# The exponential of the later routing softmaxes: GpSimd raises e to a power, in place of ScalarE's Exp

## The chip, the cores and the metric

One core of a Trainium2 chip runs the whole kernel. The metric is the device time of one execution in microseconds (us). Three runs of the kernel before are shown, and one execution was profiled.

## What is computed

Four residual layers on x of shape (4, 512, 128), each behind a layer norm: a gated power attention, a mixture of experts, a gated linear recurrence (HGRN), and the same mixture of experts again. The change lies in the routing of the mixtures. Cut to that:

```python
scores = softmax(xf @ gate_w.T, axis=-1)          # 8 experts
_, sel = top_k(scores + expert_bias, 2)
top_scores = take_along_axis(scores, sel, axis=1)
# rows sorted by expert; routed = x[token] * score
h = silu(routed @ w1[e]) * (routed @ w3[e])
out = zeros.at[token].add(h @ w2[e])
```

## The kernel before, in words

The 2048 tokens are worked in halves of 1024. A mixture layer on one half is one **set of jobs**, so there are four sets, m = 0 to 3 (two layers by two halves). A set has 23 jobs; a job is 128 gathered rows of one expert. All four sets run in one unrolled stream of 92 jobs (`for J in range(...)`, with `m, s = divmod(J, 23)`; s is the job's slot in its set).

One job goes through the engines like this. GpSimd gathers the 128 rows (`gather_pool`, L1518), twelve buffers deep. TensorE turns them (L1583), multiplies by w1 (L1614) and w3 (L1617). ScalarE takes silu of the first product (`silu_scalar`, L1693), VectorE multiplies it with the second product (`mix_vector`, L1757), TensorE turns the result (L1579), ScalarE copies what was turned (L1595), TensorE multiplies by w2 (L1634), ScalarE takes the product out of PSUM (L1700), and GpSimd returns it by an indirect DMA to the tokens' places (`return_pool`, L1526), eight buffers deep. TensorE's w1 product of a job waits until silu of the job before has emptied its bank, and silu of job J stands in ScalarE's queue ahead of the take-out of job J - 2.

Every engine works strictly in the order in which its instructions are written. What isn't part of a job is put between jobs by hand, by tables of slots (`IN_FIRST`, `IN_SECOND`, `IN_THIRD`): `between_tensor`, `between_vector`, `between_scalar` and `between_pool` are called behind each job and issue what their table has for that slot.

While set m runs, the routing of set m + 1 is prepared in this way. On VectorE the stages stand in the order `softmax` (L1370, L1371: the maximum over 8 experts and the subtraction, on the logits that TensorE left by L1322, a tile L8 of 128 x 64), `top` (L1374 to L1377: sum, reciprocal, product, bias), `first` and `second` (the two largest), and then ranks, slots and row numbers for the gathers. Between `softmax` and `top` stands the exponential: in the kernel before, `prepare_scalar(m, "exp")` on ScalarE (L1345), which waits for `s_rd` from VectorE and signals `s_re`, for which `top` waits. There are three such **places** within the jobs: in set 0 at slot 8 (`top` stands one slot later, behind the next job's L1757), in set 1 at slot 18, and in set 2 at slot 15 (there `softmax`, `top` and `first` all stand in the one slot, ahead of the next job's L1757). The exponential of the very first routing is made earlier, amid the attention layer, and isn't touched.

GpSimd's own stream within the jobs is, for each job, its return, then `between_pool`, then the gathers that are due. `norm_root` (L196) and `rms_pool` (L1945) there raise variances to the power -0.5 on tiles of 128 x 4; both are tensor_tensor with the operation pow.

`const_pool` makes the constants at the start; `s_const` counts them up to `NCONST`, for which VectorE waits before the first softmax and GpSimd before `key_rows_pool(True)`.

Of the kernel before, what the change touches and what calls it, by code (L numbers as in the profile page):

```python
# [1 line left out]

# [7 lines left out]
ALU = mybir.AluOpType  # L10
# [4 lines left out]
P = 128  # L15
# [8 lines left out]
NE, HID = 8, 352  # L24
# [3 lines left out]
HT = NT // 2  # L28
# [39 lines left out]
def build(nc, x, W, Wi, Wf, Wg, conv_i, conv_f, gnw, Wo, gate_w, ebias, w1, w2, w3, out):  # L68
# [8 lines left out]
    with ExitStack() as ctx:  # L77
        def sb(name, shape, dt=F32):
            return ctx.enter_context(nc.sbuf_tensor(name, shape, dt))

        def sem(name):
            return ctx.enter_context(nc.semaphore(name))
# [14 lines left out]
        carry1 = sb("carry1", [P, NE, HT])  # L97
        zeros = sb("zeros", [P, C])
        mhalf = sb("mhalf", [P, HT])
        iolane = sb("iolane", [P, P])  # L100
        idhi = sb("idhi", [P, 1])
        idlo = sb("idlo", [P, TOPK, HT])
# [15 lines left out]
        s_const = sem("s_const")  # L118
# [17 lines left out]
        def link(ins, who="dve"):  # L136

            count[who] += 1
            engine, done = own[who]
            ins.then_inc(done, 1)  # L140
            engine.wait_ge(done, count[who])

        def bc(ap, shape):
            return ap.to_broadcast(shape)
# [9 lines left out]
        def norm_turn(n, b):  # L154

            return norm_number(n, b) + 1

        def batch(b):
            return slice(TB * b, TB * b + TB)

        def by_scalar(n, b):
            return n == 1 and b < 3
# [29 lines left out]
        def norm_root(n, b):  # L192

            g = nc.gpsimd
            g.wait_ge(s_var, norm_turn(n, b))
            ins = g.tensor_tensor(lnr[:, batch(b)], lnv[:, batch(b)], mhalf[:, 0:TB], ALU.pow)  # L196
            if by_scalar(n, b):
                link(ins, who="pool")
                ins = g.tensor_tensor(shift[:, batch(b)], mneg[:, batch(b)], lnr[:, batch(b)], MUL)
            ins.then_inc(s_std, 1)  # L200
# [29 lines left out]
        def turn_scalar(n, b, bank):  # L230
            a = nc.scalar
            a.wait_ge(s_xTp, norm_number(n, b) + 1)
            a.activation(xT[:, 512 * b:512 * b + 512], ps[:, bank, :], ACT.Copy).then_inc(s_xT, 1)
# [5 lines left out]
        L8 = sb("L8", [P, HT, NE])  # L239
# [52 lines left out]
        def key_rows_pool(odd):  # L292

            g = nc.gpsimd
            if not odd:
# [4 lines left out]
                return  # L300
            g.wait_ge(s_const, NCONST)
            g.wait_ge(s_vzp, B)
# [106 lines left out]
        def unit_of(b):  # L409
            return 0 if b == 0 else 1  # L410

        NCONST = 17
        PARTS = 8
        STORES = 16 * 8

# [122 lines left out]
        def const_pool():  # L538
            g = nc.gpsimd

            def part1(t, v):
                link(g.memset(t[:], v), who="pool")

            def triangle(t, op, fill, base, pattern, cm):
                g.affine_select(out=t[:], in_=t[:], compare_op=op, fill=fill, base=base,
                                pattern=pattern, channel_multiplier=cm).then_inc(s_const, 1)

            part1(ident, 0.0)
            triangle(ident, ALU.not_equal, 1.0, 0, [[-1, P]], 1)
            part1(tri, 1.0)  # L550
            triangle(tri, ALU.is_ge, 0.0, 0, [[1, P]], -1)
            g.memset(zeros[:, :], 0.0).then_inc(s_const, 1)
            g.memset(onesb[:, :], 1.0).then_inc(s_const, 1)
            g.memset(ones[:, :], 1.0).then_inc(s_const, 1)
            g.memset(va[:, :, :, HS:VW], 1.0).then_inc(s_const, 1)
            link(g.memset(mhalf[:, :], -0.5), who="pool")
            norm_root(0, 0)
            part1(identb, 0.0)
            triangle(identb, ALU.not_equal, 1.0, 0, [[-1, P]], 1)
            part1(negmask, 0.0)  # L560
            triangle(negmask, ALU.is_ge, NEG, 0, [[0, TB], [1, P]], -1)
            for b in range(1, B):
                norm_root(0, b)
            key_rows_pool(False)
            part1(trib, 1.0)
            triangle(trib, ALU.is_ge, 0.0, -1, [[1, P]], -1)
            g.iota(iom8[:, :], [[1, NE]], base=-8, channel_multiplier=0, allow_small_or_imprecise_dtypes=True).then_inc(s_const, 1)
            g.iota(iojob[:, :], [[1, JOBS]], base=0, channel_multiplier=0, allow_small_or_imprecise_dtypes=True).then_inc(s_const, 1)
            g.iota(io128[:, :], [[P, HT]], base=0, channel_multiplier=0, allow_small_or_imprecise_dtypes=True).then_inc(s_const, 1)
            g.iota(iolane[:, :], [[1, P]], base=0, channel_multiplier=0, allow_small_or_imprecise_dtypes=True).then_inc(s_const, 1)  # L570
            g.iota(idhi[:, :], [[1, 1]], base=HT * TOPK, channel_multiplier=HT * TOPK, allow_small_or_imprecise_dtypes=True).then_inc(s_const, 1)
            g.iota(idpad[:, :], [[P, JOBS]], base=HT * TOPK * (P + 1), channel_multiplier=1, allow_small_or_imprecise_dtypes=True).then_inc(s_const, 1)
            g.iota(idlo[:, :, :], [[1, TOPK], [TOPK, HT]], base=0, channel_multiplier=0, allow_small_or_imprecise_dtypes=True).then_inc(s_const, 1)
            part1(carry1, 1.0)
            g.memset(carry1[:, :, 0:1], 0.0).then_inc(s_const, 1)
            key_rows_pool(True)
            for n in range(NOFF):
                decayed_pool(0, n)
# [582 lines left out]
        def heads_pool():  # L1161
            g = nc.gpsimd
            for G in range(GROUPS):
                for r in range(GH):
# [38 lines left out]
        s_rd = sem("s_rd")  # L1203
        s_re = sem("s_re")
# [53 lines left out]
        IN_FIRST = {'stats': 4, 'apply': 6, 'turn': 7, 'logits': 8, 'softmax': 8, 'exp': 8, 'top': 9, 'first': 10, 'second': 11,  # L1258
                    'ranks': 12, 'weigh': 12, 'slots': 13, 'spread': 15, 'lanes': (15, 16), 'number': 17, 'ids': 17, 'experts': 19,
                    'taps': 19, 'root': 1, 'high': 16}  # L1260
# [80 lines left out]
        def prepare_scalar(m, stage):  # L1341
            a = nc.scalar
            if stage == "exp":
                a.wait_ge(s_rd, m + 1)
                a.activation(L8[:], L8[:], ACT.Exp).then_inc(s_re, 1)  # L1345
            if stage == "high":
                a.wait_ge(s_eq, m + 1)
                a.activation(injobid[:, :, 0, :], injob[:], ACT.Copy, scale=idhi[:, 0:1]).then_inc(s_in, 1)

        def prepare_vector(m, stage):  # L1350
# [12 lines left out]
            if stage == "softmax":  # L1363

                v.wait_ge(s_lgp, m + 1)
                if m == 0:
                    v.wait_ge(s_eb, 16)
                    v.wait_ge(s_const, NCONST)
                lgt = ps[:, BK_X, 0:64].rearrange("p (t e) -> p t e", e=NE)
# [350 lines left out]
        def between_scalar(m, s):  # L1720
            if m == 0:
                at = IN_FIRST
                if s == at["turn"]:
                    turn_scalar(1, 3, BK_X)
            elif m < 3:
                at = IN_LATER[m]
                for k in range(2):
                    b = 2 * m - 2 + k
                    if s == at["tanh"][k]:
                        tanh_scalar(b)  # L1730
                    if s == at["silu"][k]:
                        silu_in_scalar(b)
                    if s == at["taken x"][k]:
                        turn_scalar(2, b, BK_X)
                for k in range(2):
                    b = 2 * m - 2 + k
                    if s == at["taps"][k]:
                        taps_scalar(b)
                    if s == at["squares"][k]:
                        squares_scalar(b)  # L1740
                    if s == at["taken y"][k]:
                        turn_scalar(3, b, BK_X)
            else:
                return
            if s == at["exp"]:
                prepare_scalar(m + 1, "exp")
            if s == at["high"]:
                prepare_scalar(m + 1, "high")

# [136 lines left out]
        def silu_in_scalar(b):  # L1886
            a = nc.scalar
            a.wait_ge(s_ci, b + 1)
            a.activation(si[:, b % 2, :], ui[:, b % 2, :], ACT.Silu).then_inc(s_si, 1)
# [57 lines left out]
        def output_vector(b):  # L1947
# [3 lines left out]
            for t in range(TB):  # L1951
                i = TB * b + t
                v.scalar_tensor_tensor(xt[:, i, :], ps[:, out_bank(b), P * t:P * t + P], rms[:, b, t:t + 1], xt[:, i, :], MUL, ADD).then_inc(s_xr, 1)

        def between_pool(m, s):

            if m == 0 and s == IN_FIRST["root"]:
                norm_root(1, 3)
            if m in (1, 2):
                at = IN_LATER[m]  # L1960
                for k in range(2):
                    b = 2 * m - 2 + k
                    if s == at["root x"][k]:
                        norm_root(2, b)
                    if s == at["root y"][k]:
                        norm_root(3, b)
                for k in range(2):
                    if s == at["rms"][k]:
                        rms_pool(2 * m - 2 + k)
# [158 lines left out]
```

## Time and profile before

| What | Value |
| --- | --- |
| median of three runs | 557.98 us (557.59 to 559.41) |
| the profiled execution's own time | 556.64 us |
| its span, from first to last instruction | 554.9 us |
| granted TensorE clock, mean over the span | 0.901 |

The span leaves out 1.7 us that lie around it in the execution's time. In the profile PE is TensorE, DVE is VectorE, ACT is ScalarE and POOL is GpSimd. "Idle before <- X" is the time that an engine stood before an instruction, and what ended it; "remote" and "another core or an unknown queue" mean that the profile found no instruction for the signal, and the ends of matmuls are modelled.

### The profile page before, as it was taken

The page shows a single profiled execution, that of the slowest core. Times are in us where ns is not written, and L with a number is a line of the kernel's source. Part 1 is how long each engine was busy: PE and PEld are TensorE (multiplying, and loading weights), DVE is VectorE, ACT ScalarE, POOL GpSimd, SP SyncE. Part 2 cuts the span into 40 slices and gives each one's busy share as a digit, 9 for nine tenths or more (in the row PEclk, how much of TensorE's full clock was granted, in tenths as well). Part 3 has the DMA queues.
Part 4 walks back from the last instruction along what each step waited for, and adds up shares of the span by engine and source line. Part 5 has one row for each costly group of instructions (what it writes and reads, how often), then busy time and mean ns, then how long its engine had stood idle before and what let it go on. Part 6 is the DMA issues. An engine that isn't in the chain of part 4 may idle for free.

```text
span 554.9 us, 11008 instructions
## 1 busy us (share of the span) xinstructions
PE 439.5 (79%) x3822; PEld 325.7 (59%) x3822; DVE 336.7 (61%) x800; ACT 323.2 (58%) x557; POOL 310.1 (56%) x333
## 2 busy tenths in 40 slices
PE   4777997887787686986997989974998769789790
PEld 2554675565575463765675658752676657567570
DVE  6979889959779892414731868373887284132121
ACT  2486899898797685444554565551674443354450
POOL 5253576655554278374566567626566726566541
PEclk9787899989897799897999899885999977898985
DMA  6343560570589403021413112323111331232204
GB/s 152 96 113 62 131 123 15 137 122 8 137 233 204 80 17 77 20 62 34 73 46 117 30 43 46 66 58 119 30 39 41 66 62 37 84 116 46 41 29 128
DMA packets 47760, 43.55 MB, mean 78 GB/s; under 512 B 10100, under 2 KB 43692, under 8 KB 47684
## 3 DMA queue, kind: packets, MB, share of 16 engines
q1 hardware_dynamic: 41820, 30.73, 23.4%
q0 software_dynamic: 5888, 12.12, 9.8%
q8 instruction: 33, 0.54, 0.4%
q14 instruction: 19, 0.16, 0.1%
HBM read 25.95 MB, written 15.89 MB: 75 GB/s over the span
## 4 chain that ended last, share of the span: by engine, by line
PE 47%; DVE 18%; ACT 10%; issue 9%; another core or an unknown queue 8%; DMA 4%; SPq 2%; POOL 0%; DVEq 0%; ACTq 0%; POOLq 0%
PE ps L1634 9%; PE ps L1617 8%; PE ps L1614 8%; PE ps L1579 4%; DVE A L1036 4%; PE ps L981 2%; ACT PP L1111 2%; PE ps L1583 2%; ACT E L1120 2%; PE ps L935 2%; DMA QS<-gates 1%; PE ps L993 1%; DVE xh L210 1%; PE ps L618 1%
## 5 line engine op out<-in xcount | busy, mean ns | idle before, releaser
L1526 POOL DMA_INDIRECT token_out<-ysb,id_out x92 | 91.8, 998 | 94.2 <-ACT ysb L1700 76.0
L1757 DVE SCALAR_TENSOR_TENSOR hid<-silu,tiled,ps 128x352 f32<-128x352 f32 x92 | 53.2, 578 | 127.2 <-PE ps L1617 75.9
L1170 POOL TENSOR_TENSOR PP<-PP,E 128x512 f32<-128x512 f32 x64 | 82.3, 1287 | 65.7 <-ACT PP L1111 65.5
L1518 POOL DMA_INDIRECT tiled<-scaled_rows,id_in x92 | 92.9, 1009 | 28.1 <-issue 23.2
L1111 ACT ACTIVATE PP<-A,feps 128x1024 f32<-128x1024 f32 x80 | 93.3, 1167 | 15.5 <-DVE A L1036 15.4
L1036 DVE TENSOR_SCALAR A<-ps 128x1024 int32<-128x1024 int32 x76 | 91.2, 1219 | 16.7 <-PE ps L935 15.1
L1595 ACT ACTIVATE turned<-ps 128x512 f32<-128x512 f32 (+2 forms) x98 | 55.9, 571 | 73.0 <-PE ps L1583 44.1
L1634 PE MATMUL ps<-room,turned 128*128 x552 | 82.1, 287 | 13.4 <-ACT ysb L1700 12.0
L1614 PE MATMUL ps<-room,turned 128*128 x184 | 78.2, 509 | 14.9 <-ACT silu L1693 13.8
L1634 PEld LDWEIGHTS ps<-room,turned 128*128 128x128 f32 x552 | 73.2, 202 | 16.5 <-issue 16.5
L1617 PE MATMUL ps<-room,turned 128*128 x184 | 75.7, 495 | 0.0
L1693 ACT ACTIVATE silu<-ps,tiled 128x352 f32<-128x352 f32 x92 | 50.9, 553 | 35.1 <-PE ps L1614 27.5
L935 PE MATMUL ps<-QS,KS 102*128 102x128 bf16 (+2 forms) x448 | 53.5, 258 | 13.8 <-DVE A L1036 9.4
L1579 PEld LDWEIGHTS ps<-ident,hid 128*128 128x128 f32 x276 | 37.0, 150 | 42.4 <-issue 27.3
L1579 PE MATMUL ps<-ident,hid 128*128 128x128 f32 x276 | 48.8, 288 | 12.1 <-DVE hid L1757 5.6
L935 PEld LDWEIGHTS ps<-QS,KS 102*128 102x128 bf16 x448 | 34.0, 104 | 30.4 <-DVE A L1036 12.7
L1617 PEld LDWEIGHTS ps<-room,turned 128*128 128x128 f32 x184 | 38.0, 207 | 22.5 <-issue 5.0
L1700 ACT ACTIVATE ysb<-ps 128x128 f32<-128x128 f32 x92 | 25.5, 277 | 34.5 <-remote 18.1
L1614 PEld LDWEIGHTS ps<-room,turned 128*128 128x128 f32 x184 | 30.2, 204 | 18.8 <-issue 18.7
L1120 ACT ACTIVATE E<-ps 128x512 f32<-128x512 f32 x64 | 38.6, 603 | 2.5 <-PE ps L965 2.2
L1583 PE MATMUL ps<-ident,tiled 128*128 128x128 f32 x92 | 26.9, 293 | 7.9 <-DMA tiled<-scaled_rows,id_in 7.1
L981 PE MATMUL ps<-PP,vp 128*9 128x128 f32 x768 | 27.1, 291 | 1.2 <-issue 1.2
(225 smaller groups left out, 627.2 us busy)
## 6 DMA issues: line engine op xcount, KB each, us to landing
parts<-room SPq DMA_DIRECT2D x32, 128.0 KB, 2.4
yb<-token_out SPq DMA_DIRECT2D x8, 512.0 KB
QS<-parts SPq DMA_DIRECT2D x21, 192.0 KB
KS<-parts SPq DMA_DIRECT2D x21, 192.0 KB
room<-in_L_ffn_w_dram SPq DMA_DIRECT2D x2, 1408.0 KB, 7.9
scaled_rows<-xh SPq DMA_DIRECT2D x4, 516.0 KB
scaled_rows<-xh SPq DMA_DIRECT2D x8, 256.0 KB
tiled<-scaled_rows,id_in POOLq DMA_INDIRECT x92
```

Source lines behind the costliest of these rows:

```text
L935: return pe.matmul(bank[:, col:col + width], KS[:, slot, h, P * j:P * j + P], QS[:, slot, h, t0:t0 + width], start=True, stop=True)
L1036: v.tensor_scalar(A[:, U % 3, :].bitcast(I32), ps[:, bank:bank + 2, :].rearrange("p k t -> p (k t)").bitcast(I32), 0x7fffffff, None, ALU.b ...
L1111: a.activation(PP[:, G % 2, 2 * p:2 * p + 2, :].rearrange("p k t -> p (k t)"), A[:, U % 3, :], ACT.Square, bias=feps[:, G // NG:G // NG + ...
L1170: g.tensor_tensor(w, w, E[:, hh % 4, :], MUL).then_inc(s_PD, 1)
L1518: g.indirect_dma_start(rows[:, J % ROWS, :], None, xs_d[m], bass.IndirectOffsetOnAxis(ap=id_in[:, m % 2, s:s + 1], axis=0)).then_inc(s_row ...
L1526: g.indirect_dma_start(yr_d[m], bass.IndirectOffsetOnAxis(ap=id_out[:, m % 2, s:s + 1], axis=0), ysb[:, J % OUTS, :], None).then_inc(s_ret ...
L1579: ins = pe.transpose(ps[:, BK_R, P * c:P * c + P], hid[:, J % 2, P * c:P * c + P], ident[:, :])
L1595: a.activation(turned[:, n % 2, c0:c1, :].rearrange("p c l -> p (c l)"), ps[:, BK_R, P * c0:P * c1], ACT.Copy).then_inc(s_t, 1)
L1614: pe.matmul(ps[:, BK_A, 0:HID], turned[:, n % 2, 3, :], w13[:, bass.ds(e, 1), 0, :].squeeze(1), start=True, stop=True).then_inc(s_AB, 1)
L1617: pe.matmul(ps[:, BK_B + J % 2, 0:HID], turned[:, n % 2, 3, :], w13[:, bass.ds(e, 1), 1, :].squeeze(1), start=True, stop=True).then_inc(s_ ...
L1634: ins = pe.matmul(ps[:, BK_Y, 0:P], turned[0:hw, n % 2, c, :], w2s[0:hw, bass.ds(e, 1), c, :].squeeze(1), start=(c == 0), stop=(c == len(H ...
L1757: v.scalar_tensor_tensor(hid[:, J % 2, 0:HID], silu[:, J % 2, :], rows[:, J % ROWS, C:CW], ps[:, BK_B + J % 2, 0:HID], MUL, MUL).then_inc( ...
```

## The change

The three exponentials within the jobs leave ScalarE. GpSimd gets a column of 128 constants e, and a function that waits for `s_rd`, raises e to the power of L8, in place, and signals `s_re`. It stands in GpSimd's stream behind the return of the job three slots ahead of the table's `exp` slot, and ahead of that job's gathers. The rest of the streams is as it was.

```diff
+        euler = sb("euler", [P, 1])
...
-        NCONST = 17
+        NCONST = 18
...
             part1(carry1, 1.0)
+            g.memset(euler[:, :], math.e).then_inc(s_const, 1)
             g.memset(carry1[:, :, 0:1], 0.0).then_inc(s_const, 1)
...
             else:
                 return
-            if s == at["exp"]:
-                prepare_scalar(m + 1, "exp")
             if s == at["high"]:
                 prepare_scalar(m + 1, "high")
...
+        def exp_pool(m):
+
+            g = nc.gpsimd
+            g.wait_ge(s_rd, m + 1)
+            g.tensor_tensor(L8[:], bc(euler[:, 0:1].unsqueeze(2), [P, HT, NE]), L8[:], ALU.pow).then_inc(s_re, 1)
+
         def between_pool(m, s):
 
             if m == 0 and s == IN_FIRST["root"]:
                 norm_root(1, 3)
+            if m < 3 and s == (IN_FIRST, IN_SECOND, IN_THIRD)[m]["exp"] - 3:
+                exp_pool(m + 1)
```

## Rows read from the trace of the kernel before

**Rows 1.** The page, part 1: busy time, share of the span, instructions.
```profile
PE 439.5 (79%) x3822; PEld 325.7 (59%) x3822; DVE 336.7 (61%) x800; ACT 323.2 (58%) x557; POOL 310.1 (56%) x333
```

**Rows 2.** The page, part 4: the chain that ended last, by engine.
```profile
PE 47%; DVE 18%; ACT 10%; issue 9%; another core or an unknown queue 8%; DMA 4%; SPq 2%; POOL 0%; DVEq 0%; ACTq 0%; POOLq 0%
```

**Rows 3.** Groups of ScalarE by line: count, busy us, mean ns, idle before.
```profile
L1693 ACT ACT_TABLE_LOAD x4 | 5.1, 1283 | 0.1
...
L1345 ACT ACT_TABLE_LOAD x3 | 3.8, 1283 | 0.1
```

**Rows 4.** Timeline, first place: start us, us, engine, line, operation, idle before.
```profile
244.53 0.84 PE L1614 MATMUL ps<-room,turned 128*128 x2
...
247.88 1.28 ACT L1345 ACT_TABLE_LOAD   x1
...
251.24 0.23 DVE L1370 TENSOR_REDUCE m<-ps 128x8 f32<-128x64 f32 x1 [7.49 <-remote]
...
251.76 0.26 ACT L1345 ACTIVATE L<-L 128x64 f32<-128x64 f32 x1 [2.59 <-DVE L L1371]
...
253.33 0.55 ACT L1693 ACTIVATE silu<-ps,tiled 128x352 f32<-128x352 f32 x1
...
254.02 1.54 PE L1614 MATMUL ps<-room,turned 128*128 x2 [5.08 <-ACT silu L1693]
...
254.41 0.21 DVE L1374 TENSOR_REDUCE m<-L 128x8 f32<-128x64 f32 x1
...
255.16 0.22 DVE L1377 TENSOR_TENSOR V<-L,ebt 128x64 f32<-128x64 f32 x1
...
256.87 0.58 DVE L1757 SCALAR_TENSOR_TENSOR hid<-silu,tiled,ps 128x352 f32<-128x352 f32 x1 [1.49 <-PE ps L1617]
```

**Rows 5.** Timeline, second place.
```profile
359.83 0.26 ACT L1345 ACTIVATE L<-L 128x64 f32<-128x64 f32 x1 [1.88 <-DVE L L1371]
...
360.12 0.22 DVE L1374 TENSOR_REDUCE m<-L 128x8 f32<-128x64 f32 x1 [0.32 <-ACT L L1345]
...
362.67 0.58 DVE L1757 SCALAR_TENSOR_TENSOR hid<-silu,tiled,ps 128x352 f32<-128x352 f32 x1
...
363.99 0.85 PE L1579 MATMUL ps<-ident,hid 128*128 128x128 f32 x3
```

**Rows 6.** Timeline, third place.
```profile
444.08 0.26 ACT L1345 ACTIVATE L<-L 128x64 f32<-128x64 f32 x1 [5.55 <-issue]
...
444.37 0.22 DVE L1374 TENSOR_REDUCE m<-L 128x8 f32<-128x64 f32 x1 [0.32 <-issue]
...
446.92 0.58 DVE L1757 SCALAR_TENSOR_TENSOR hid<-silu,tiled,ps 128x352 f32<-128x352 f32 x1
...
448.84 0.85 PE L1579 MATMUL ps<-ident,hid 128*128 128x128 f32 x3
```

**Rows 7.** Groups of GpSimd by line and form, columns as in rows 3.
```profile
L1170 POOL TENSOR_TENSOR PP<-PP,E 128x512 f32<-128x512 f32 x64 | 82.3, 1287 | 65.7 <-ACT PP L1111 65.5
L196 POOL TENSOR_TENSOR lnr<-lnv,mhalf 128x4 f32<-128x4 f32 x16 | 16.5, 1031 | 18.8 <-DVE lnv L190 18.1 <-issue 0.7
...
L304 POOL MEMSET xh<- 96x256 f32 x2 | 0.8, 390 | 15.2 <-PE ps L627 15.2
...
L199 POOL TENSOR_TENSOR shift<-mneg,lnr 128x4 f32<-128x4 f32 x3 | 0.6, 203 | 0.2
```

**Rows 8.** Stretches around the first place: TensorE's granted clock is the column PEclk.
```profile
core 0: us, PE busy (x) PEld busy (x) DVE busy (x) ACT busy (x) POOL busy (x), PEclk, DMA share, GB/s
...
249.00:254.00 5.00, 0.00 (x0) 0.00 (x0) 0.53 (x3) 2.38 (x5) 1.10 (x2) 0.61 0.17 26
254.00:257.00 3.00, 2.98 (x7) 1.88 (x8) 1.41 (x6) 1.09 (x3) 1.88 (x2) 0.51 0.09 27
```

**Rows 9.** Timeline of GpSimd ahead of the third place.
```profile
439.88 0.98 POOL L1518 DMA_INDIRECT tiled<-scaled_rows,id_in  x1 [0.30 <-issue]
...
442.45 0.98 POOL L1518 DMA_INDIRECT tiled<-scaled_rows,id_in  x1 [0.30 <-issue]
```

More of the change, by code:

```diff
@@ L1 @@
 from contextlib import ExitStack
+import math
 import concourse.bass as bass
```

## The prediction

> **What bounds the kernel now.** The page's busy times come first. TensorE is busy for 79% of the span, ScalarE for 58%, GpSimd for 56% [rows 1]. The chain that ended last lies on TensorE for 47%, on VectorE for 18%, on ScalarE for 10% and on GpSimd for nothing [rows 2]. So ScalarE's busy time is worth little as an average, and what counts is what stands still at the three places where the exponential is made. The groups of ScalarE show a table load ahead of each of the three exponentials and one ahead of the silu behind it, 1.283 us each; the fourth load at silu's line is the first of all jobs and stays [rows 3]. The view has no load at the tanh between the jobs, so tanh and silu share a table, and with the exponentials gone all six loads go: 7.7 us of ScalarE.
>
> The timelines of the three places tell what that is worth. At the first, ScalarE loads the exponential's table at 247.88 and is then idle until VectorE has its maximum (251.24) and its difference; the exponential starts at 251.76, the next job's silu only at 253.33, and TensorE's w1 product of the job after it at 254.02, after 5.08 us idle [rows 4]. The first of the two loads is thus hidden in a wait. What is on the path is ScalarE's exponential, the second load, and the wait itself, since silu stands behind it. At the second and third places VectorE goes on at once with `top` and `first`, and reaches the next job's product at 362.67 and 446.92, with no gap that the exponential left it; TensorE turns that product at 363.99 and 448.84 [rows 5, 6]. There VectorE sets the pace, and VectorE waits for the exponential.
>
> **The change, part by part.** What decides is D, the time of GpSimd's power on 128 x 64. The trace has powers on 128 x 4 alone: 16 of them, 1031 ns in the mean; a product on the same 128 x 4 takes 203 ns and one on 128 x 512 takes 1287 ns [rows 7].
>
> *D from below.* If everything that the power costs above the product were paid once, each further column would cost what the product's does, (1287 - 203) / 508 = 2.1 ns, and D = 1.03 + 60 x 0.0021 = 1.16 us. *D from above.* If all 1031 ns were paid per column, D = 1.031 / 4 x 64 = 16.5 us. *What I take.* The product's 203 ns hold nearly no work, so they are the price of an instruction; the other 1031 - 203 = 828 ns are the power itself, done for 4 columns, 207 ns each. A power is a long run of arithmetic for each value, and nothing in the rows points to a preparation that is paid once. So D = 0.2 + 64 x 0.207 = 13.5 us, against 0.26 us of the exponential on ScalarE.
>
> *First place.* The power starts when the exponential did, at 251.76. VectorE's `top` starts at 251.76 + D + 0.03 and takes from 254.41 to 255.38 = 0.97; the product behind it, at 256.87 before [rows 4], comes at 252.79 + D (with hand-overs of 0.03), which is D - 4.1 later: +9.4 us. The w1 product that the next silu needs was issued at 244.53, and ScalarE came to the exponential at 247.88; but VectorE, which waits for logits that TensorE computed ahead of that product, was let go only at 251.24, so TensorE's signals came late here and silu could have started at about 251.3, in place of 253.33. That is worth 2.0 us, and only where D is short; with D = 13.5 the next product on VectorE has to wait anyway.
>
> *Second place.* `top` comes at 359.83 + D + 0.03, before at 360.12: D - 0.26 later. The product at 362.67 moves with it and ends at 363.25 + D - 0.26; TensorE turned it at 363.99, 0.71 behind a hand-over of 0.03. So TensorE is D - 0.97 later: +12.5 us [rows 5].
>
> *Third place.* In the same way `top` moves by D - 0.26, and of the product's end (447.50) to 448.84 a gap of 1.31 is taken up: D - 1.57, +11.9 us [rows 6].
>
> *Sum.* 3 D - 6.6 = 33.9 us. Nothing hides it: VectorE waits in its own order, `hid` is two deep, so TensorE stops a job later, and the last chain runs through it. Each place delays all that follows, as there is no wait for anything outside this chain that was there before and could shrink by so much.
>
> *GpSimd's queue.* Behind the exponential stand the next returns and gathers. Ahead of the third place GpSimd issues back to back, with 0.30 us between one issue and the next, as at 439.88 and 442.45 [rows 9]; these now stand behind the power. While it runs the jobs stand still as well, so rows and buffers (twelve and eight deep) are not used up; I cost this at nothing. With a short D it is a rival, below. The memset of 128 x 1 at the start is less than the 390 ns of a 96 x 256 one, and GpSimd waits 15.2 us for TensorE right behind it [rows 7]: nothing.
>
> *The clock.* TensorE was granted 0.61 on average while it stood still (249 to 254) and 0.51, its 1.2 GHz level, in the 3 us after [rows 8]. This is there before; a longer stand may add about 1 us at each place, and I leave it to the range.
>
> *A rule against the rows.* Between the exponential's end at 252.02 and silu's start at 253.33 lies 1.31 us, the load and nothing else [rows 4]. The Trainium skill ("ScalarE: Activation LUTs", What ACT_TABLE_LOAD costs) gives 1283 ns for the load and some 1380 ns for a drain besides, 2.66 us for a switch. By that rule silu's gain at the first place would be 3.4 us in place of 2.0; the trace doesn't agree.
>
> The profiled execution took 556.64 us, 1.3 under the median of the runs shown, 557.98. Its own sum is 556.64 + 33.9 = 590.5, and against the median 591.9, so **592**.
>
> **The rivals.** *The power is paid once (D = 1.16).* First place -2.0, second +0.19, third -0.41: -2.2 us, 555.8. This is the case on the other side. By the sum 3 D - 6.6 it turns at D = 2.2: below, the change gains. For it speaks that 1031 ns is odd as four columns' work if the engine is at all wide; against it that no row shows a fixed price on GpSimd over 0.2 us. The Trainium skill ("GPSIMD Engine Reference", Performance versus the Vector engine) gives about 2.6 cycles at 1.2 GHz per element of an operation with two inputs, without an exception for power. By that rule the case is this one; the trace agrees for the product and not, at four columns, for the power. If silu could go on when ScalarE came to the exponential (247.88) and not at 251.3, the first place would give 5.4 and the time would be 552.4.
>
> *Part of it is overlapped between columns.* With a third of the slope, 0.07 us a column, D = 1.03 + 60 x 0.07 = 5.2 and the sum is +9.0: 567. Anything between 558 and 588 belongs here.
>
> *GpSimd's queue with a short D.* At the third place the gather of 439.88 goes out at about 445.3, 5.4 us later. If TensorE has to wait for its rows by all of that, -2.2 turns into +3.2: 561. Against it: the rows are for jobs several slots on, and the place itself stands still for part of that time.
>
> That the loads stay (another function needing the other table) is shut out by rows 3.
>
> **How the numbers follow.** About 0.3% (1.7 us) is what a measurement of this kernel can tell from no change. The power per column: 0.55. Partly overlapped: 0.20. Paid once: 0.20, of which 0.14 lies over 0.3% faster (D under 1.4) and 0.06 within. The queue: 0.05, most of it slower. So faster 0.15, same 0.09, slower 0.76. The likeliest case has its own range, from D = 12.5 (589) to D = 16.5 (601). The range to hold the time 8 in 10 reaches down to where the partly overlapped cases and some of the flat ones end, 557, and up to 600.
>
> **What would show it.** In the profile after, ScalarE has one table load within the jobs in place of seven (5.1 and 3.8 us of rows 3 become 1.3). The line of the power appears on GpSimd with three instructions on 128 x 64, and their mean is D: 13.5 us proves the forecast, about 1.2 the rival. VectorE's L1374 is idle before for 3 x (D + 0.03), less the 0.6 to 1.2 us of the product that stands ahead of it at the first place. TensorE stands still for 10 us or more at each place. A mean of D under 2.2 us would make the prediction wrong in its sign; a D near 13.5 with a total far from +34 would mean that a wait elsewhere took the stall up, and rows of gathers that come late at the third place would speak for the queue.

## The result, and the profile after

The kernel after takes 581.67 us in the median (579.79 to 583.21, 4 runs) beside 558.59 for the kernel before on the same chip (557.59 to 559.41, 4 runs): a ratio of 1.0456 [1.0408, 1.0503]. The medians lie 23.1 us apart, the ratio makes it 25.5, and the profiled execution took 581.9 us, 25.3 more than that of before. Some executions of a kernel take over 1.5% longer than its fastest; the ratios leave them out, so the amounts of the experiments below are taken from the ratios, but the profiles of the product's and the half width's kernels (555.49 and 569.44 us) are of such executions.

GpSimd's group of the power, which the kernel before does not have (line, engine, operation, tiles; busy us, mean ns; idle before and its releaser):

```profile
L1961 POOL TENSOR_TENSOR L<-euler,L 128x64 f32<-128x64 f32 x3 | 31.6, 10549 | 5.9 <-DVE L L1375 5.9
```

So **D is 10.55 us**; the three executions differ by 2 ns. Who stood still for it is said by the one line of VectorE's `top`, as its source view has it (four executions, the first is the unchanged first half):

```profile
L1378 DVE TENSOR_REDUCE m<-L x4: 219/220/221, 162.2 to 473.2; 128x8 f32<-128x64 f32 x4
its engine sat idle before it (us, times) until:
  POOL L L1961: 30.9, 3
  ACT L L1349: 0.3, 1
```

Of 31.6 us of power, VectorE was idle for 30.9; the rest is the one product ahead of it at the first place. The page's busy times and its chain, to be read against [rows 1, 2]:

```profile
PE 443.3 (76%) x3804; PEld 330.6 (57%) x3822; DVE 336.4 (58%) x800; ACT 315.2 (54%) x548; POOL 341.0 (59%) x337
...
PE 45%; DVE 18%; another core or an unknown queue 9%; ACT 8%; issue 8%; POOL 6%; DMA 4%; SPq 2%; DVEq 0%; POOLq 0%; ACTq 0%
```

GpSimd is up by 30.9 us of busy time, ScalarE down by 8.0 (three exponentials and six loads are 8.5). GpSimd, at 0% of the chain before, now holds 6% of it. The loads went as foreseen: silu's line keeps the first one, and the line of the exponential that stays on ScalarE, L1349, has none:

```profile
L1697 ACT ACT_TABLE_LOAD x1 | 1.3, 1283 | 0.0
```

The timelines of the places, beside [rows 4 to 6] (start us, us, engine, line, operation, idle before). The first:

```profile
246.57 0.22 DVE L1374 TENSOR_REDUCE m<-ps 128x8 f32<-128x64 f32 x1 [1.95 <-remote]
...
246.99 0.56 ACT L1697 ACTIVATE silu<-ps,tiled 128x352 f32<-128x352 f32 x1
...
247.14 10.55 POOL L1961 TENSOR_TENSOR L<-euler,L 128x64 f32<-128x64 f32 x1 [2.20 <-DVE L L1375]
247.58 0.58 DVE L1759 SCALAR_TENSOR_TENSOR hid<-silu,tiled,ps 128x352 f32<-128x352 f32 x1 [0.52 <-ACT silu L1697]
...
257.72 0.22 DVE L1378 TENSOR_REDUCE m<-L 128x8 f32<-128x64 f32 x1 [9.56 <-POOL L L1961]
...
258.74 0.58 DVE L1759 SCALAR_TENSOR_TENSOR hid<-silu,tiled,ps 128x352 f32<-128x352 f32 x1
...
259.46 0.88 PE L1583 MATMUL ps<-ident,hid 128*128 128x128 f32 x3 [4.94 <-DVE hid L1759]
...
267.83 0.28 ACT L1704 ACTIVATE ysb<-ps 128x128 f32<-128x128 f32 x1 [3.17 <-remote]
...
270.80 0.58 DVE L1759 SCALAR_TENSOR_TENSOR hid<-silu,tiled,ps 128x352 f32<-128x352 f32 x1 [5.93 <-remote]
...
273.55 0.60 ACT L1599 ACTIVATE turned<-ps 128x512 f32<-128x512 f32 x1 [3.72 <-remote]
```

The power starts 4.6 us earlier than the exponential did (the jobs ahead of it are 0.68 us early), because VectorE waits 1.95 us for its logits in place of 7.49. Silu, with no load and no exponential ahead of it, goes at 246.99. TensorE stands still for only 4.94 us here, no longer than the 5.08 of before. The product behind `top` is at 258.74, against 256.87. So the power as such costs little at this place. Another 7 us are lost between 264 and 279, most of them in waits that the profile calls "remote": it places no instruction to the signal. The second place:

```profile
369.53 10.55 POOL L1961 TENSOR_TENSOR L<-euler,L 128x64 f32<-128x64 f32 x1 [1.87 <-DVE L L1375]
...
380.11 0.22 DVE L1378 TENSOR_REDUCE m<-L 128x8 f32<-128x64 f32 x1 [10.68 <-POOL L L1961]
...
382.66 0.58 DVE L1759 SCALAR_TENSOR_TENSOR hid<-silu,tiled,ps 128x352 f32<-128x352 f32 x1
...
383.39 0.87 PE L1583 MATMUL ps<-ident,hid 128*128 128x128 f32 x3 [12.25 <-DVE hid L1759]
```

VectorE waits 10.68 us and TensorE behind it 12.25. The third place has the same shape:

```profile
462.58 10.55 POOL L1961 TENSOR_TENSOR L<-euler,L 128x64 f32<-128x64 f32 x1 [1.83 <-DVE L L1375]
...
473.16 0.22 DVE L1378 TENSOR_REDUCE m<-L 128x8 f32<-128x64 f32 x1 [10.67 <-POOL L L1961]
...
475.71 0.58 DVE L1759 SCALAR_TENSOR_TENSOR hid<-silu,tiled,ps 128x352 f32<-128x352 f32 x1
...
476.44 0.88 PE L1583 MATMUL ps<-ident,hid 128*128 128x128 f32 x3 [12.26 <-DVE hid L1759]
```

The waits for the logits, in the source view of the kernel before:

```profile
L1370 DVE TENSOR_REDUCE m<-ps x4: 223/225/225, 162.0 to 443.6; 128x8 f32<-128x64 f32 x4
its engine sat idle before it (us, times) until:
  remote: 21.1, 3
```

and in that of the kernel after:

```profile
L1374 DVE TENSOR_REDUCE m<-ps x4: 223/224/226, 161.4 to 462.0; 128x8 f32<-128x64 f32 x4
its engine sat idle before it (us, times) until:
  remote: 11.4, 3
```

In the timelines these waits are 7.49, 5.88 and 7.76 us before, and 1.95, 4.58 and 4.85 after. Three stretches of the kernel after, one for each place, in the columns of [rows 8]:

```profile
277.00:280.00 3.00, 3.00 (x11) 2.13 (x10) 0.91 (x3) 0.72 (x2) 0.98 (x1) 0.51 0.07 22
...
371.00:380.00 9.00, 0.14 (x1) 0.00 (x0) 0.00 (x0) 0.14 (x1) 9.00 (x1) 0.56 0.00 0
...
476.00:480.00 4.00, 3.56 (x14) 3.07 (x15) 3.60 (x15) 0.87 (x2) 3.09 (x4) 0.50 0.37 51
```

From 371 to 380 nothing but the power runs, save the last 0.14 us of a matmul and of an activation. TensorE's granted clock is 0.56 in that time and 0.50, its 1.2 GHz level, in the 4 us after the third place. So the clock is down behind a stand, as it was before. New is the stretch behind the late signals of the first place: from 270 to 280 the clock is at 0.50 to 0.51, where the kernel before has, in the same jobs:

```profile
266.00:270.00 4.00, 4.00 (x27) 3.12 (x26) 2.44 (x10) 1.98 (x4) 2.93 (x3) 1.00 0.88 134
```

Slots 14 and 15 lie 4.20 us apart there, against 2.29 in undisturbed jobs at full clock, so of the 7 us about 1.9 are the clock (an estimate from these two).

**By place.** The same products of VectorE are compared in the two timelines. Between slot 7 and slot 15 of the first set the lag, after less before, goes from -0.68 to +9.17 us (269.88 to 279.05): +9.85. At the second place it goes from +10.94 to +19.99 (362.67 to 382.66): +9.05. At the third it goes from +21.36 to +28.79 (446.92 to 475.71): +7.43. Between the places the lag grows by 1.8 and 1.4 us, and behind the third it falls by 3.3, to 25.45. The first place is thus the dearest, where the forecast had it the cheapest.

### The profile page after: what moved, and what is told of

Read it like the earlier page. It is cut to its first block, busy times and chain, and to the rows that moved or that the text cites. A ratio compares the mean times of both kernels' runs of the same rounds, so it can differ in the third digit from the quotient of the medians.

```text
span 580.2 us, 10985 instructions
## 1 busy us (share of the span) xinstructions
PE 443.3 (76%) x3804; PEld 330.6 (57%) x3822; DVE 336.4 (58%) x800; ACT 315.2 (54%) x548; POOL 341.0 (59%) x337
## 4 chain that ended last, share of the span: by engine, by line
PE 45%; DVE 18%; another core or an unknown queue 9%; ACT 8%; issue 8%; POOL 6%; DMA 4%; SPq 2%; DVEq 0%; POOLq 0%; ACTq 0%
PE ps L1638 9%; PE ps L1618 8%; PE ps L1621 7%; POOL L L1961 5%; PE ps L1583 4%; DVE A L1040 4%; PE ps L1587 2%; PE ps L985 2%; PE ps L939 2%; ACT E L1124 2%; ACT PP L1115 2%; PE ps L1852 1%; DMA QS<-gates 1%; PE ps L1007 1%
## 5 line engine op out<-in xcount | busy, mean ns | idle before, releaser
L1638 PE MATMUL ps<-room,turned 128*128 x552 | 84.8, 294 | 12.7 <-ACT ysb L1704 10.8
L1638 PEld LDWEIGHTS ps<-room,turned 128*128 128x128 f32 x552 | 75.8, 208 | 15.3 <-issue 15.2
L1583 PE MATMUL ps<-ident,hid 128*128 128x128 f32 x276 | 49.6, 292 | 43.4 <-DVE hid L1759 33.7
L1618 PE MATMUL ps<-room,turned 128*128 x184 | 79.4, 516 | 3.1 <-ACT silu L1697 2.2
L1583 PEld LDWEIGHTS ps<-ident,hid 128*128 128x128 f32 x276 | 37.1, 151 | 75.0 <-issue 57.9
L1621 PE MATMUL ps<-room,turned 128*128 x184 | 76.0, 497 | 0.0
L1621 PEld LDWEIGHTS ps<-room,turned 128*128 128x128 f32 x184 | 38.4, 209 | 23.2 <-issue 6.2
L939 PEld LDWEIGHTS ps<-QS,KS 102*128 102x128 bf16 x448 | 34.6, 106 | 29.5 <-DVE A L1040 11.7
L1704 ACT ACTIVATE ysb<-ps 128x128 f32<-128x128 f32 x92 | 25.5, 277 | 37.0 <-remote 16.8
L1961 POOL TENSOR_TENSOR L<-euler,L 128x64 f32<-128x64 f32 x3 | 31.6, 10549 | 5.9 <-DVE L L1375 5.9
L1618 PEld LDWEIGHTS ps<-room,turned 128*128 128x128 f32 x184 | 30.9, 208 | 6.6 <-issue 6.6
L1587 PE MATMUL ps<-ident,tiled 128*128 128x128 f32 x92 | 27.1, 295 | 6.3 <-DMA tiled<-scaled_rows,id_in 5.5
```

The lines of the kernel that those rows point to most:

```text
L939: return pe.matmul(bank[:, col:col + width], KS[:, slot, h, P * j:P * j + P], QS[:, slot, h, t0:t0 + width], start=True, stop=True)
L1583: ins = pe.transpose(ps[:, BK_R, P * c:P * c + P], hid[:, J % 2, P * c:P * c + P], ident[:, :])
L1618: pe.matmul(ps[:, BK_A, 0:HID], turned[:, n % 2, 3, :], w13[:, bass.ds(e, 1), 0, :].squeeze(1), start=True, stop=True).then_inc(s_AB, 1)
L1621: pe.matmul(ps[:, BK_B + J % 2, 0:HID], turned[:, n % 2, 3, :], w13[:, bass.ds(e, 1), 1, :].squeeze(1), start=True, stop=True).then_inc(s_ ...
L1638: ins = pe.matmul(ps[:, BK_Y, 0:P], turned[0:hw, n % 2, c, :], w2s[0:hw, bass.ds(e, 1), c, :].squeeze(1), start=(c == 0), stop=(c == len(H ...
L1961: g.tensor_tensor(L8[:], bc(euler[:, 0:1].unsqueeze(2), [P, HT, NE]), L8[:], ALU.pow).then_inc(s_re, 1)
```

## The experiments

The theory was that VectorE, waiting in its own order, pays D at each place, by the three terms. The rivals for the size were GpSimd's queue (gathers and returns behind the power) and GpSimd's work slowing others. The first four kernels shared the runs of the kernel before, whose median was 554.99 us there.

**One place at a time.** The exponential goes back to ScalarE everywhere but at one place; `BY_POOL` is (0,), (1,) or (2,):

```
+        BY_POOL = (0,)
...
+            if s == at["exp"] and m not in BY_POOL:
+                prepare_scalar(m + 1, "exp")
...
-            if m < 3 and s == (IN_FIRST, IN_SECOND, IN_THIRD)[m]["exp"] - 3:
+            if m in BY_POOL and s == (IN_FIRST, IN_SECOND, IN_THIRD)[m]["exp"] - 3:
```

First place:

> The power on GpSimd at the first place alone, ScalarE's exponential at the other two. The power measured 10.55 us. Theory (VectorE stands in its own order for the power, and the forecast's terms hold with D = 10.55): +6.4 us over the kernel before, so about 565. Rival (what costs is GpSimd's queue, held for 10.55 us, with the returns and gathers behind it): GpSimd isn't backed up here, so near 0 to -2, about 557.

Measured: 567.10 us, 1.0222 [1.0173, 1.0271], **+12.3**.

Second place:

> The power at the second place alone. Theory: D - 1.0 = +9.6 us, about 568. Rival (GpSimd's queue): all gathers of the set are out by then, only returns wait, so near 0, about 558.

Measured: 565.29 us, 1.0210 [1.0143, 1.0276], **+11.7**.

Third place:

> The power at the third place alone. Theory: D - 1.6 = +9.0 us, about 567.5. Rival (GpSimd's queue): this is the one place where GpSimd issues back to back, so it carries most of the 23 us, 15 or more, about 573. If the three singles add up to about 23 to 25 the places are independent.

Measured: 561.11 us, 1.0105 [1.0054, 1.0156], **+5.8**. GpSimd's timeline there:

```profile
442.17 10.55 POOL L1964 TENSOR_TENSOR L<-euler,L 128x64 f32<-128x64 f32 x1 [1.85 <-DVE L L1376]
452.92 1.01 POOL L1523 DMA_INDIRECT tiled<-scaled_rows,id_in  x1 [0.20 <-issue]
454.23 1.00 POOL L1531 DMA_INDIRECT token_out<-ysb,id_out  x1 [0.30 <-issue]
```

The queue does pile up behind the power: six gathers and returns follow at 1.3 us from start to start. The rival's forecast here was 15 us or more. Yet this place is the cheapest, so the queue costs nothing that shows, and that rival falls. In the kernel after, too, TensorE's wait for rows did not grow; the groups of L1587 after and of the same line, L1583, before end in

```profile
L1587 PE MATMUL ps<-ident,tiled 128*128 128x128 f32 x92 | 27.1, 295 | 6.3 <-DMA tiled<-scaled_rows,id_in 5.5
```

and 7.9 us, 7.1 of it for DMA. The three singles sum to 29.8 us, where all together cost 25.5. The second place holds its term of 9.6 in its interval (7.9 to 15.3 us); the first lies 5.9 over its 6.4 and the third 3.2 under its 9.0, both outside. In the profiles of these three kernels, the lag steps by 9.4 (slots 7 to 15), 9.0 and 7.5 us at the place that has the power, as in the kernel after. So the places don't act on each other; what each single kernel has more or less than its step lies elsewhere in the run.

They show one thing more. The kernels of the second and third place keep ScalarE's exponential at the first, and yet wait there for the logits for only

```profile
244.77 0.23 DVE L1375 TENSOR_REDUCE m<-ps 128x8 f32<-128x64 f32 x1 [2.92 <-remote]
```

and 2.42 us (at 246.66), where the kernel before waits 7.49. Up to there they differ from it only by the constant e. So at the first place the shorter wait doesn't come from the engine that makes the exponential; no kernel tried the constant alone. At the second and third places the wait does go with it: it is 4.5 to 5.0 us in every profile of these three kernels, of the one after, and of the product's and the half width's below, where GpSimd has the place, and 5.9 to 9.0 us where ScalarE has it (on the chips of the first three comparisons).

**The same order, next to no work.** A product in place of the power; this kernel leaves the exponential of the later halves out.

```
-            g.tensor_tensor(L8[:], bc(euler[:, 0:1].unsqueeze(2), [P, HT, NE]), L8[:], ALU.pow).then_inc(s_re, 1)
+            g.tensor_tensor(L8[:], bc(euler[:, 0:1].unsqueeze(2), [P, HT, NE]), L8[:], MUL).then_inc(s_re, 1)
```

> The kernel after with a product in place of the power in all three instructions (128 x 64, expected 0.34 us each): same queues, waits and signals, no exponential, so the routing weights and choices aren't the reference's. Theory: the cost is D alone, and with D = 0.34 the terms give -2.0 - 0.6 - 1.2 = -3.8 us, about 554.5. Rival (the place in GpSimd's order costs by itself, since its wait holds returns and gathers back): 0 or above, 558 to 562.

Measured: 546.97 us, 0.9857 [0.9807, 0.9907], **-7.9**. GpSimd's group:

```profile
L1961 POOL TENSOR_TENSOR L<-euler,L 128x64 f32<-128x64 f32 x3 | 0.9, 286 | 5.9 <-DVE L L1375 5.9
```

At 0.29 us in place of 10.55 the same hand-over is a gain. So it is the power's length that costs, not where it stands. The gain is twice what the terms gave. VectorE's idle time ahead of the logits' maximum is 11.6 us here, as in the kernel after (11.4) and not as in the one before (21.1). That fits a ScalarE that doesn't stand at the exponential, but at the first place, 1.92 us here, the single kernels above speak against it. As the values of the routing differ too, a gain from other routing choices isn't shut out. From this one to the kernel after, 3 x (10.55 - 0.29) = 30.8 us of GpSimd's time cost 33.4 (7.9 + 25.5), about one for one.

**Half the width.** The power on four of the eight rows of tiles; the other half gets no exponential.

```
-            g.tensor_tensor(L8[:], bc(euler[:, 0:1].unsqueeze(2), [P, HT, NE]), L8[:], ALU.pow).then_inc(s_re, 1)
+            g.tensor_tensor(L8[:, 0:4], bc(euler[:, 0:1].unsqueeze(2), [P, 4, NE]), L8[:, 0:4], ALU.pow).then_inc(s_re, 1)
```

> The power on half of the tile at all three places (128 x 32; the other 32 columns stay as differences, without an exponential, so the routing of their tokens isn't the reference's). If the power is paid per column beyond a small fixed part, D = 0.40 + 32 x 0.159 = 5.5 us (from 1.03 at 4 columns and 10.55 at 64), and between the product's -8 us (D = 0.29) and the +23 of D = 10.55 the time falls on a line: -8 + 5.2 x 3.03 = +7.7 us, about 563. Rival (the price comes in blocks of columns, or is the same for 32): D near 10 and about +20.

Measured, beside 552.54 us for the kernel before: 566.47 us, 1.0226 [1.0181, 1.0270], **+12.5**.

```profile
L1961 POOL TENSOR_TENSOR L<-euler,L 128x32 f32<-128x32 f32 x3 | 16.3, 5443 | 5.4 <-DVE L L1375 5.4
```

Twice the width costs 5.11 us more, 160 ns a column, with 0.3 to 0.4 left over. Between these widths the price is paid per column, as forecast. The time of the whole misses its forecast: it lies 4.8 us above the +7.7 that was forecast from the line between the product's kernel and the one after, and 2.8 above the sum at this D, 9.7. In the profile the lag steps by 4.4, 4.3 and 2.2 us at the three places; at the first, the product behind `top` is 2.8 us early, and 7.2 us are lost behind it, as in the kernel after.

**`top` put later, with and without the power.** If the cost is VectorE's wait in its own order, it must go once VectorE has products to do in that time. If a long power slows others, it stays. Both kernels move the stages of the first set, and the second has the power at the first place besides (the `BY_POOL` edit above):

```
-        IN_FIRST = {... 'exp': 8, 'top': 9, 'first': 10, 'second': 11,
-                    'ranks': 12, 'weigh': 12, 'slots': 13, ...
+        IN_FIRST = {... 'exp': 8, 'top': 12, 'first': 12, 'second': 13,
+                    'ranks': 14, 'weigh': 14, 'slots': 15, ...
```

> The kernel before, with `top` and what follows it at the first place moved to later slots (top and first 12, second 13, ranks and weigh 14, slots 15; spread and the rest as before). All exponentials on ScalarE. It is the control for the next run: within 2 us of the kernel before by either theory.

Measured: 559.50 us, 1.0102 [1.0059, 1.0145], **+5.6**.

> The same slots, with the power on GpSimd at the first place. Theory (the cost is VectorE standing in its own order in front of `top`): four jobs run while the power does, so of the +12 us of e1 nearly all goes: 0 to +2 over e6. Rival (GpSimd itself held for 10.55 us, or its use of SBUF beside VectorE): the cost stays, +8 to +12 over e6.

Measured: 559.00 us, 1.0100 [1.0066, 1.0135], **+5.5**. The timeline of the second:

```profile
245.95 10.55 POOL L1964 TENSOR_TENSOR L<-euler,L 128x64 f32<-128x64 f32 x1 [2.02 <-DVE L L1376]
246.01 0.58 DVE L1762 SCALAR_TENSOR_TENSOR hid<-silu,tiled,ps 128x352 f32<-128x352 f32 x1
247.87 0.58 DVE L1762 SCALAR_TENSOR_TENSOR hid<-silu,tiled,ps 128x352 f32<-128x352 f32 x1 [1.27 <-PE ps L1622]
250.16 0.58 DVE L1762 SCALAR_TENSOR_TENSOR hid<-silu,tiled,ps 128x352 f32<-128x352 f32 x1 [1.71 <-PE ps L1622]
252.45 0.58 DVE L1762 SCALAR_TENSOR_TENSOR hid<-silu,tiled,ps 128x352 f32<-128x352 f32 x1 [1.71 <-PE ps L1622]
...
256.54 0.22 DVE L1379 TENSOR_REDUCE m<-L 128x8 f32<-128x64 f32 x1 [3.50 <-POOL L L1964]
```

Four products go by while the power runs, the last three 2.29 us apart, as in undisturbed jobs. The power that cost 12.3 us at this place costs nothing against the same slots with ScalarE (5.5 and 5.6 us, to within some 3 us by the two intervals). So the cost is VectorE's wait in its own order, and a GpSimd that works for 10.55 us isn't what slows the others here. But to put `top` later costs 5.6 us by itself. The control was forecast within 2 us of the kernel before, and that failed. In the timeline the products of the second kernel run up to 9 us ahead of those of the kernel before (slot 12), and this is given back by slot 16, behind a late signal for `ysb`, which reads what TensorE computed:

```profile
273.66 0.28 ACT L1705 ACTIVATE ysb<-ps 128x128 f32<-128x128 f32 x1 [6.50 <-remote]
```

**No table loads, no GpSimd.** The same value on ScalarE from tanh, which shares silu's table, with e^x = (1 + t)/(1 - t) and t = tanh(x/2):

```
-                a.activation(L8[:], L8[:], ACT.Exp).then_inc(s_re, 1)
+                a.activation(L8[:], L8[:], ACT.Exp if m == 0 else ACT.Tanh, scale=1.0 if m == 0 else 0.5).then_inc(s_re, 1)
...
+                if m:
+                    link(v.tensor_scalar(Q8[:], L8[:], -1.0, 1.0, MUL, ADD))
+                    link(v.reciprocal(Q8[:], Q8[:]))
+                    link(v.scalar_tensor_tensor(L8[:], L8[:], 1.0, Q8[:], ADD, MUL))
```

> Exponential on ScalarE as (1 + t) / (1 - t) with t = tanh(x / 2), which is in silu's table: no table load within the jobs, three more VectorE instructions of about 0.22 us at each place, ScalarE still waits for VectorE's difference ahead of silu. If the two loads were what the product of e4 saved: -3 to -8 us. If it was ScalarE no longer standing in front of silu: near 0 (+0.7 of VectorE at the second and third places, -1.3 at the first).

Measured: 554.48 us, 1.0000 [0.9966, 1.0034], nothing to within 1.9 us, as the second of the two readings had it. Six table loads (7.7 us of ScalarE) are gone and three times some 1.1 us of VectorE have come: busy for 0.19, 0.55 and 0.23 us, with gaps between them. In the profile the lag steps by -1.0 us at the first place and by +1.2 and +1.0 at the other two. So the loads are worth 1 to 2 us at the first place, and nothing at the second and third, where VectorE's new instructions cost what they take. VectorE's wait for the logits is 21.1 us here, as before, with ScalarE still at the exponential. So the loads by themselves are not the product's gain.

**ScalarE freed without GpSimd.** So the exponential was put behind the next job's silu, once as it is and once by tanh (with the edits above):

```
+            if m < 3 and s == (IN_FIRST, IN_SECOND, IN_THIRD)[m]["exp"] + 1:
+                prepare_scalar(m + 1, "exp")
...
-            if s == at["exp"]:
-                prepare_scalar(m + 1, "exp")
```

> The kernel before with ScalarE's Exp moved behind the next job's silu at each of the three places, table loads and all. Theory (what the product of e4 saved, 8 us, was silu no longer standing behind the exponential): silu goes early, but the load of 1.28 us is now on VectorE's way to `top` at the second and third places (+1.3 to +2 each) and silu of the job after it waits for the load back: -4 to +1. Rival (moving it changes nothing, as the loads are the cost): within 1.5 us of before.

Measured: 508.86 us, 1.0068 [1.0035, 1.0101], **+3.4**.

> The tanh form of e8, behind the next job's silu: no table load and no wait of ScalarE ahead of silu. Theory: it takes what the product took, less three VectorE instructions (0.75 us) and silu's 0.55 at the second and third places, so -8 + 2.5 = about -5 us. Rival (e4 gained by leaving out the exponential's work or by other routing choices, not by silu's place): within 1.5 us of the kernel before, as e8.

Measured: 508.56 us, 1.0050 [1.0013, 1.0086], **+2.5**.

This chip ran the kernel before in 505.70 us. Both kernels are slower than it, and the gain forecast for the second, 5 us, is not there. The waits of the first of the two on VectorE:

```profile
DVE m L1370 <- PE ps L1322: 8.2, 4, 3.0
DVE m L1374 <- ACT L L1345: 6.0, 4, 2.4
```

The logits are waited for 8.2 us in four times, all put down to TensorE, and no wait of this profile is "remote". The kernel before, profiled on the same chip with the powers of the last experiment added at its start, waits 8.7 us for them, so here nothing shows that ScalarE's place matters to the logits. What silu may gain, VectorE loses at `top`: 6.0 us, against 1.0 in that profile. As the late signals that the edit was to remove are not there on this chip, it decided nothing about them. The tanh kernel ran once more, to see it where the late signals are:

> The kernel of e10 once more. In e10 the kernel before took 505.7 us, and no wait there ends by a signal that the profile can't place; in e1 to e8 it took 553 to 555, with some 60 us of such waits. If the same chip as in e9 to e11 is drawn (before near 506): +0.5% again. If one like those of e1 to e8 is drawn (before near 555): theory (the 8 us of e4 were TensorE's late signals, which shrink when ScalarE no longer stands in front of silu) -4 to -8 us; rival (e4's gain came with the exponential left out) within 1.5 us.

Measured: 509.73 us beside 505.89, 1.0062 [1.0025, 1.0099]: the same kind of chip again, and inconclusive for its purpose.

**The power by itself.** In the constants of the kernel before, powers of several widths were added:

```
+            for n in (1, 2, 8, 16, 32):
+                link(g.tensor_tensor(pout[:, 0:n], bc(pone[:, 0:1], [P, n]), pexp[:, 0:n], ALU.pow), who="pool")
+            link(g.tensor_tensor(pout[:, 0:16], pone[:, 0:16], bc(mhalf[:, 0:1], [P, 16]), ALU.pow), who="pool")
```

> The kernel before with powers of 1, 2, 8, 16 and 32 columns (e to the -1.7), and one of 16 columns with the exponent -0.5, added on GpSimd at the start, where it would wait for TensorE. Paid per column: 0.397 + 0.159 n gives 0.56, 0.71, 1.67, 2.93, 5.47 us, and the last again 2.93. Rival (blocks of columns): 1 and 2 columns cost the 1.03 us of 4. Rival (the price hangs on the numbers): the last differs from the fourth.

Measured, in GpSimd's groups by form (`pexp` is -1.7, `mhalf` is -0.5):

```profile
L582 POOL TENSOR_TENSOR pout<-pone,pexp 128x32 f32<-128x32 f32 x1 | 5.8, 5820 | 0.1
...
L583 POOL TENSOR_TENSOR pout<-pone,mhalf 128x16 f32<-128x16 f32 x1 | 2.9, 2895 | 0.1
L582 POOL TENSOR_TENSOR pout<-pone,pexp 128x16 f32<-128x16 f32 x1 | 2.9, 2893 | 0.1
L582 POOL TENSOR_TENSOR pout<-pone,pexp 128x8 f32<-128x8 f32 x1 | 2.1, 2145 | 0.1
...
L582 POOL TENSOR_TENSOR pout<-pone,pexp 128x1 f32<-128x1 f32 x1 | 0.9, 855 | 0.1
L582 POOL TENSOR_TENSOR pout<-pone,pexp 128x2 f32<-128x2 f32 x1 | 0.8, 795 | 0.1
```

The forecasts were 0.56, 0.71, 1.67, 2.93 and 5.47 us: right at 16 columns and low elsewhere. From one column to four (1.03 us) the time moves by 0.24 us at most; from there it grows with the width, at eight columns 0.47 us above the line. The exponents -1.7 and -0.5 give the same at 16 columns. At 32 the kernel's own logits took 5.44 and this constant 5.82, which no run explains.

## Why the prediction was right, and where its sizes were off

**D.** The forecast's reading, a price per column, held from four columns up, and "the power is paid once" fell. Its size was off. The step that failed is "the other 1031 - 203 = 828 ns are the power itself, done for 4 columns, 207 ns each". The measured line is (10.549 - 1.031) / 60 = 159 ns a column with 0.40 us fixed, twice the 203 ns taken, and one column, at 855 ns, costs nearly what four cost. This put 3 x (13.5 - 10.55) = 8.9 us too much into the sum. A row of a second width was missing; 855 ns for a single column would have shown it. "Part of it is overlapped" named the right direction, at 5.2 us far too short. By the forecast's own division, the measured time lies in that rival's stretch (558 to 588) and under the range of the likeliest case (589 to 601); it is the range for the time, 557 to 600, that held.

**The sum.** 3 D - 6.6 with the measured D is 25.0 us, against 25.3 between the two profiled executions and 25.5 by the ratio (23.1 between the medians). The total agrees, the parts do not, and the agreement is in part luck: 8.0 us less by sooner logits and 7.3 us more by late signals, both left out of the forecast, nearly cancel.

**When the power starts.** Beside the size of D this is the step that failed: "The power starts when the exponential did", and with it "there is no wait for anything outside this chain that was there before and could shrink by so much". The exponential starts at 251.76, 359.83 and 444.08, the power at 247.14, 369.53 and 462.58, and the jobs ahead of it have lags of -0.68, +10.94 and +21.36 us. So against its jobs the power started 3.9, 1.2 and 2.9 us sooner, as the waits for the logits had shrunk. With this put in, the forecast's chain on VectorE is right at each place: D - 4.1 - 3.9 = 2.5 at the first, and D - 0.26 less 1.2 and 2.9, 9.05 and 7.4, at the others; measured were 2.55, 9.05 and 7.43.

**First place.** The forecast's "D - 4.1" is 6.4 at the measured D. The profile shows 9.85 and the kernel with this place alone 12.3. Of the 9.85, only 2.55 (the lag from -0.68 to +1.87) are there at the product behind `top`. The other 7.3 are lost 5 to 20 us later, to late signals and, by some 1.9, to the clock behind them. "TensorE stands still for 10 us or more at each place" holds at two, with 12.25 and 12.26, and not here.

**ScalarE's gain.** "Worth 2.0 us, and only where D is short" was too small. The product in the power's place gained 7.9 us over three places where the terms gave about 4. It was read from one idle stretch of one timeline, and at the second and third places nothing was given for ScalarE's order, while the logits came sooner there wherever GpSimd had the exponential. In the profile of the product's kernel the lag steps by -1.2, -1.0 and -2.8 us at the three places, 5.0 of the 7.9.

**Second and third place.** D - 0.97 is 9.6, measured 9.05 in the profile and 11.7 alone, within its interval: near, though not by its own working, as it counts 0.71 us that TensorE takes up and not the 1.2 us by which the logits came sooner. D - 1.57 is 9.0, measured 7.43 and 5.8: too much, and of that the logits, sooner by 2.9 us, are the part that the profile shows.

**GpSimd's queue at nothing** was right, by the third place and the unchanged wait for rows. **The clock left to the range** held: its two levels are where they were, and about 1 us at each place was allowed for. At the first place it took some 1.9 us, behind the late signals.

**The table loads** are gone as foreseen and are worth little, as the tanh kernel shows. Of the longer switch of "ScalarE: Activation LUTs" in the Trainium skill (What ACT_TABLE_LOAD costs), no run here showed a sign; the 1.31 us of [rows 4] stand. The Trainium skill's 2.6 cycles an element ("GPSIMD Engine Reference", Performance versus the Vector engine) were the rule beside the rival that fell: worked out from them, 128 x 64 is an estimated 0.14 us above the start. The product's 0.29 us agrees and the power's 10.55 does not.

**What stays open** is where the "remote" waits come from, and with them three things: why 7.3 us are lost behind the first place, why the wait for the logits there is 7.49 us in the kernel before and 2.4 to 2.9 in two kernels with the same order up to there, and whether the product's 7.9 us are there only on chips that have these waits, or in part come from the routing that it changes. Neither that kernel nor the change itself was tried on the chip without them. No kernel that computes the whole was shown to be faster than the one before; the one with the added widths, which only adds work, took 501.55 us in a single run beside 505.70 (23 runs, 501.72 to 508.06), and that says how far one run can be off.

## What to carry to other kernels

Price a power on GpSimd by the column: 0.4 us and 0.16 us for each column of 128 partitions, 10.55 us at 64, and 0.8 to 1.0 us for one to four. Take no such price from one narrow width. When work goes to an idle engine, ask who waits for it in order: here all but 0.7 of 31.6 us came back as VectorE's wait, and one of the three powers was free where the consumer's stage stood three slots later, though that move had its own price, 5.6 us. Count a table load as a gain only where it is not hidden in a wait: here the loads of one place in three were worth something. A moved instruction starts when its input comes, and that time can move too: compare it with the jobs around it, not with the clock of the old timeline.

## What the runs showed of the hardware

- One and the same kernel took 558.6, 555.0 and 552.5 us in the first three comparisons (that of the change among them), and 505.7 and 505.9 in the last two, on other chips. There TensorE was busy for 417.0 us (in the kernel with the exponential behind silu) in place of some 440, and no wait ended "remote". In the profile of the kernel before, 59 us of waits did: 21.1 for the logits, 18.1 at `ysb`, 15.2 at `turned`, 4.6 at `hid`. In that of the kernel after 73.6 us did, though the part for the logits fell to 11.4.
- Where these waits stand changes from kernel to kernel. At the first place VectorE waited 7.49 us in the kernel before and 1.95 in the one after, and 5.93 at `hid` some 20 us later; two kernels with the order of the one before up to there waited 2.92 and 2.42.
- On GpSimd a power to -0.5 costs what one to -1.7 costs (2.9 us at 16 columns), and one column costs 855 ns where two cost 795.
